# One more step between the up and the down matmuls of an expert tile, TensorE's loop turned each 24 tiles, and the expert output in four PSUM banks

## The reference, cut to what matters

```python
x = x + xattn(layernorm(x), ctx)                # per batch of 128 rows
xt = layernorm(x)                               # 2048 tokens
scores = softmax(xt @ Wg.T)                     # 16 experts; 2 of 4 groups, then the top 4
combine = the scores of the 4 chosen experts
h = silu(xt @ W1[e].T) * (xt @ W3[e].T)         # 176 hidden features
y = sum over e of combine[:, e] * (h @ W2[e].T)
z = silu(xt @ Ws1.T) * (xt @ Ws3.T) @ Ws2.T     # 352 shared hidden features
return x + y + z
```

## Time and profile before

| | us |
|---|---|
| median of 3 executions | 466.83 |
| lowest, highest | 464.65, 470.10 |
| the profiled execution | 459.79 |
| its span, first to last instruction | 457.8 |
| first up matmul of the expert pass | 256.9 |
| start of the last y on ScalarE | 416.4 |

### The profile page before, as it was taken

The page is one execution under the profiler, slowest core; times in us unless marked ns, Lnnn a source line. Parts: engine busy times, 40 slices in busy tenths (PEclk is TensorE's granted clock), DMA queues, the critical chain, the costliest instruction groups (busy, mean ns, idle before and its releaser), DMA issues.

```text
span 457.8 us, 9903 instructions
## 1 busy us (share of the span) xinstructions
PE 332.7 (73%) x2379; PEld 229.9 (50%) x2380; DVE 275.3 (60%) x976; ACT 210.1 (46%) x553; POOL 235.2 (51%) x284
## 2 busy tenths in 40 slices
PE   0788897977888732575099797988988798897830
PEld 0565575655566521243066465665656566574510
DVE  4488879867886883552044454555545455563686
ACT  2466765555454422331145354555555445564510
POOL 2567765588888888717500054554554445453000
PEclk9998766566555555887589999999999989999975
DMA  8713123133333342317340155555555545512994
GB/s 291 246 57 102 64 62 103 56 120 106 119 106 106 115 150 108 116 67 257 124 84 0 32 125 134 126 128 114 125 131 123 118 114 131 129 42 61 348 349 161
DMA packets 82055, 57.79 MB, mean 126 GB/s; under 512 B 58858, under 2 KB 75501, under 8 KB 82032
## 3 DMA queue, kind: packets, MB, share of 16 engines
q1 hardware_dynamic: 63600, 39.60, 30.6%
q0 software_dynamic: 6912, 17.84, 11.0%
q10 hardware_dynamic: 11520, 0.09, 1.5%
HBM read 24.58 MB, written 24.53 MB: 107 GB/s over the span
## 4 chain that ended last, share of the span: by engine, by line
PE 44%; POOL 17%; DVE 12%; issue 12%; another core or an unknown queue 5%; DMA 5%; ACT 2%; SPq 1%; DVEq 0%; POOLq 0%; ACTq 0%
PE bank L715 18%; PE bank L730 12%; POOL slot_rows L1351 6%; DVE x_all L1278 4%; PE bank L723 3%; POOL v L1331 3%; DMA x_all<-x_dram 3%; POOL r L1333 2%; PE bank L721 2%; DMA w<-ranked 2%; PE bank L597 2%; POOL x_all L1313 2%; PE bank L642 1%; PE bank L623 1%
## 5 line engine op out<-in xcount | busy, mean ns | idle before, releaser
L1378 POOL DMA_INDIRECT ranked<-ctx_all x80 | 79.1, 989 | 114.5 <-ACT ctx_all L576 75.4
L730 PE MATMUL bank<-w,hT 128*128 (+3 forms) x560 | 82.3, 280 | 11.2 <-DVE hT L1263 5.8
L715 PE MATMUL bank<-w,ctx_all 128*128 x480 | 85.5, 315 | 1.6 <-issue 1.3
L1351 POOL DMA_INDIRECT slot_rows<-rows_all,slot_k x64 | 65.4, 1021 | 25.6 <-issue 16.7
L1145 DVE SCALAR_TENSOR_TENSOR hid<-bank,silu 128x176 f32<-128x176 f32 x112 | 38.2, 341 | 67.1 <-ACT silu L528 42.9
L528 ACT ACTIVATE silu<-bank 128x176 f32<-128x176 f32 x112 | 35.4, 316 | 75.5 <-PE bank L715 32.2
L730 PEld LDWEIGHTS bank<-w,hT 128*128 128x128 f16 (+1 forms) x560 | 52.5, 100 | 29.9 <-issue 16.5
L533 ACT ACTIVATE hh<-hid 128x176 f16<-128x176 f32 x112 | 39.0, 348 | 39.4 <-DVE hid L1145 31.2
L721 PE MATMUL bank<-hal,hh 128*128 128x128 f16 x112 | 25.2, 225 | 41.5 <-DVE hh L1150 22.5
L715 PEld LDWEIGHTS bank<-w,ctx_all 128*128 128x128 f16 x480 | 43.0, 98 | 20.8 <-issue 3.4
L1263 DVE COPY hT<-bank 128x384 f16<-128x384 f16 x80 | 28.6, 357 | 36.7 <-PE bank L723 22.1
(11 more groups left out here) (139 smaller groups left out, 607.4 us busy)
## 6 DMA issues: line engine op xcount, KB each, us to landing
wst<-w_dram SPq DMA_DIRECT2D x18, 608.0 KB
w<-ranked SPq DMA_DIRECT2D x16, 512.0 KB, 8.8
slot_rows<-pad_rows SPq DMA_DIRECT2D x17, 144.0 KB
x_all<-x_dram SPq DMA_DIRECT2D x4, 512.0 KB, 7.9
out_dram<-x_all SPq DMA_DIRECT2D x4, 512.0 KB, 4.2
ctx_all<-ctx_dram SPq DMA_DIRECT2D x1, 1536.0 KB, 10.7
ctx_all<-slot_rows SPq DMA_TRANSPOSE x80
ctx_all<-slot_rows ACTq DMA_DIRECT2D x80, 1.0 KB
```

The source lines that it names most:

```text
L715: i = mm(U[j][:, 0:UP1], xt(2 * part + k), w[:, span(wcol + wpart * WH + k * UP1, UP1)], start=k == 0 and (wpart, part) == (0, 0), stop=k ...
L730: i = mm(y[:, 0:T], hT[0:rows, j, k * P:(k + 1) * P], w[0:rows, span(col, T)], start=start and n == 0, stop=stop and n == len(parts) - 1)
L1351: G.indirect_dma_start(scatter_rows, bass.IndirectOffsetOnAxis(ap=slot_k[:, b * TOPK + k:b * TOPK + k + 1], axis=0), rows32[:, b * ROW32:( ...
L1378: G.indirect_dma_start(ranked, bass.IndirectOffsetOnAxis(ap=pair(m)[1], axis=0), y_sb[:, m % YR, :], None, bounds_check=(TOPK + 1) * TOKEN ...
```

## The change

Four things change in the expert pass:

- **PE's order**: step s is now D of tile s-4, T of tile s-3, U of tile s. The drain is four steps.
- **PE's loop**: its body is 24 steps (`LONG = 3 * MR`), three passes; the other engines keep bodies of eight steps. The second `weights.load` of a pass (for the tiles four back) is still at the pass's first step alone.
- **Y has four banks**, one for each tile modulo 4, so that the drain's wait of D on y is dropped.
- **ACT** does y of tile s-4 ahead of the address load and of the high half of tile s-1 (it was y of s-3, behind it). **DVE** does the low half of s-2 ahead of the `hT` copy of s-3 (it was behind it).

```diff
-        LAG = {"hlo_ready": 3, "hT_ready": 3}
+        LAG = {"hlo_ready": 3, "hT_ready": 4}
...
-        BODY = MR
-        assert (NT - 2 * RING) % BODY == 0 and BODY % MR == 0 and NT % MR == 0 and 2 * RING == MR
-
-        def expert_pipeline(eng, step, lags=3):
+        LONG = 3 * MR
+        assert (NT - 2 * RING) % LONG == 0 and NT % MR == 0 and 2 * RING == MR
+
+        def expert_pipeline(eng, step, lags=3, body=MR):
             for s in range(2 * RING):
                 step(s, s, None)
-            with eng.Fori(2 * RING, NT - BODY + 1, BODY) as i:
-                for v in range(BODY):
+            with eng.Fori(2 * RING, NT - body + 1, body) as i:
+                for v in range(body):
...
-        U, H, Y = [TP, GP], [SP_, PT], [TS, HO]
+        U, H, Y = [TP, GP], [SP_, PT], [TS, HO, XB, LB]
...
                 if has(s, 1):
                     gate(EX, s - 1, k)
+                if has(s, 4):
+                    t = s - 4
+                    m = (step_v - 4) % YR
+                    wait(act, y_out[m], 4 * (t - m))
+                    act.wait_ge(meta_in[m], 4 * (t - m) + 16)
+                    act.wait_ge(EX["dn_mm"], t + 1)
+                    A(y_sb[:, m, :], Y[m][:, 0:T], ACT.Copy, scale=pair((step_v - 4) % MR)[0]).then_inc(EX["y_ready"], 1)
                 if has(s, 0) and step_v % 4 == 0:
                     pairs.load(s, step_v)
                 if has(s, 1):
                     hidden_high(EX, s - 1, k)
-                if has(s, 3):
-                    t = s - 3
...
-                    A(y_sb[:, m, :], Y[k][:, 0:T], ACT.Copy, scale=pair((step_v - 3) % MR)[0]).then_inc(EX["y_ready"], 1)
...
+                if has(s, 4):
+                    ready("hT_ready", 4)
+                    down(EX["dn_mm"], v % 2, Y[v], weights.of[step_v - 4], start=True, stop=True)
                 if has(s, 3):
                     ready("hlo_ready", 3)
-                    transpose_hidden(EX["ht_mm"], k)
-                if has(s, 1):
-                    m = (step_v - 1) % MR
-                    pe.wait_ge(xt_in[m], 2 * (s - 1 - m) + 16)
-                    wait(pe, EX["h_ready"], s - 2)
-                    up(EX["up_mm"], k, lambda q: xT[:, m, q, :], weights.of[step_v - 1])
-                if has(s, 3):
-                    ready("hT_ready", 3)
-                    if r is None and s >= NT:
-                        pe.wait_ge(EX["y_ready"], s - 4)
-                    down(EX["dn_mm"], k, Y[k], weights.of[step_v - 3], start=True, stop=True)
-
-            expert_pipeline(pe, estep)
+                    transpose_hidden(EX["ht_mm"], 1 - v % 2)
+                if has(s, 0):
+                    m = step_v % MR
+                    pe.wait_ge(xt_in[m], 2 * (s - m) + 16)
+                    wait(pe, EX["h_ready"], s - 1)
+                    up(EX["up_mm"], v % 2, lambda q: xT[:, m, q, :], weights.of[step_v])
+
+            expert_pipeline(pe, estep, 4, LONG)
...
+                if has(s, 2):
+                    hidden_low(EX, s - 2, v % 2, RS["hlo_ready"][(v - 2) % RING], 16)
                 if has(s, 3):
                     dve.wait_ge(EX["ht_mm"], s - 2)
                     wait(dve, EX["dn_mm"], s - 4)
                     V.tensor_copy(hT[:, k, :], H16[k]).then_inc(RS["hT_ready"][(v - 3) % RING], 16)
-                if has(s, 2):
-                    hidden_low(EX, s - 2, v % 2, RS["hlo_ready"][(v - 2) % RING], 16)
```

More of the change, by code:

```diff
@@ L569, in estep @@
                     hidden_high(EX, s - 1, k)
-                if has(s, 3):
-                    t = s - 3
-                    m = (step_v - 3) % YR
-                    wait(act, y_out[m], 4 * (t - m))
-                    act.wait_ge(meta_in[m], 4 * (t - m) + 16)
-                    act.wait_ge(EX["dn_mm"], t + 1)
-                    A(y_sb[:, m, :], Y[k][:, 0:T], ACT.Copy, scale=pair((step_v - 3) % MR)[0]).then_inc(EX["y_ready"], 1)
                 if has(s, 0):
@@ L582, in _ @@
             act.wait_ge(S["table_ready"], 1)
-            expert_pipeline(act, estep)
+            expert_pipeline(act, estep, 4)
             shared_units(act, sstep, B1, B, 1, lambda stage, n: None)
@@ L783, in estep @@
                 v = step_v % RING
-                k = (v + 1) % 2
                 def ready(name, lag):
```

## The result

The changed kernel takes 468.64 us (median of 12 runs) against 466.39 us of the kernel before in the same call: ratio 1.0079, 95% interval 1.0049 to 1.0109. The ratio is of executions outside a slower state that some fall into, so it isn't that of the medians. The kernel is slower by 0.8%, inside the 1% that the prediction called no change, and 20 us above the 449.0 that it forecast. The profiled execution spans 465.9 us, with the same 2379 matmuls.

What follows compares the result with a forecast made beforehand. The expert pass, led by PE's up and down matmuls, was taken to bound the kernel. Hidden loads 3, turns 11 and late signals 4 made 18 us less: 466.8 - 18 = 449 us, range 441 to 459.

Steps and rivals of the forecast that it cites:

- The late signals: PE's transpose signals reaching DVE's `hT` copy late, cause unknown: 8.9 us in the pass, half taken as won, 4 us.
- The pace: PE's up matmuls follow each other in 1.61 us; 80 tiles make 129 us, the pass's other 31 us can be won.
- Single loads hidden: PE's mid-pass address loads hide behind U, 0 to 0.1 us each where they cost 0.35: 3 us less.
- turns: PE's loop entry and two branches back cost 3 us together, where nine times 1.6 us made 14.4: 11 us less.
- Rival A: Low half, `hT`, `hid` and high half on DVE and ACT set the pace, 1.7 us a tile: 456 us, chance 0.15.
- Rival B: PE's single address loads aren't hidden, the sequencer needing 0.3 us more before U: 454 us, chance 0.08.
- Rival C: PE's long loop leaves the instruction buffer; two branches back fetch, 2 us each: 453 us, chance 0.08.
- case C in full: All of PE's long loop fetched late in every pass, twelve fetches in three passes: 461 to 473 us, chance 0.04.
- SP as the next bound: SP's loads need 1.50 us of its own per tile, not much below the new pace of 1.61 to 1.75.

## Why the prediction was wrong

**The step that failed is "The late signals".** It read: "Nothing in the diff names them. Bound from both sides: all stay (0 us won) or all go (8.9 us won) ... I take half, 4 us." A wait with an unknown cause was bounded as if it could only stay or go; that it could grow got 0.05 together with other cases. It grew: from 159.9 - 149.8 = 10.1 us of the pass before (8.9 was the estimate, and its size was about right) to 166.2 - 136.3 = 29.9 us after. That is 19.8 us more where the sum had 4 less, so 24 us of error in the pass; the time was off by 20. By the medians the growth is smaller, from 466.84 - 450.93 = 15.9 us to 468.64 - 438.62 = 30.0 us, as the profiled execution of the kernel before was one of its quicker ones; the sign is the same.

**What the rows could have said.** The prediction used POOL's scatters for their 983 ns and saw that y's wait for them had 6.4 us to spare. The same row gives 263.2 to 417.7 for 80 of them, 1.96 us apart, which is the pass's 159.9 / 80 = 2.0. Whatever happens once a tile has that distance, so the row alone doesn't name the scatters; a run without them does. The pass before was already at the mean distance that the scatters were never seen to go far below, 1.88 to 2.16 us in 14 kernels. The change took some 13 us of turns and loads out of PE's own time, and the scatters did not come more often; the time went into held signals.

**The pace.** 80 x 1.61 = 129 us, and what lies above it can be won: PE does stream at 1.61 us a step in every kernel with whole ups, and without scatters the pass is 136.3. Right about PE, wrong as a bound of the kernel.

**Single loads hidden, 3 us; turns, 11 us.** Right, 14 us together; without scatters the two passes differ by 13.5 us. The parts are right too, from one D to the next against 1.61 us in the runs without scatters. The mid-pass load of the kernel before costs 308.92 - 306.92 - 1.61 = 0.39 us (the prediction had 0.35), and now nothing. A turn there costs 316.72 - 313.76 - 1.61 = 1.35 us (1.6). A turn of the long loop costs 312.76 - 310.47 - 1.61 = 0.68 us and, as the down matmuls behind it take 0.73 instead of 0.55 us, 314.59 - 312.76 - 1.61 = 0.22 us more, together 0.9 (1.2). The turns were taken somewhat too dear on both sides.

**Rival A, the ring on DVE and ACT.** It didn't set the pace: steps of 1.61 us follow each other, and in the kernel without scatters they do for 37 us on end between two turns. Whether it would hold a PE that needs less than 1.61 us, as in the run with short ups, isn't shown.

**Rival B, loads not hidden.** No: the load at 311.2 has no gap beside it.

**Rival C, fetches.** 12 packets instead of 9 in the whole kernel, where case C in full had twelve in the three passes alone. The queues from 320 to 420 us of the changed kernel, all of them:

```profile
q1 hardware_dynamic: 22745, 5.48, 26.3%
q0 software_dynamic: 2400, 5.37, 15.9%
q10 hardware_dynamic: 7200, 0.05, 4.0%
```

PE's second pass ends at 367.5 us and its third at 416.6, and in both there is no fetch. So the loop of some 900 instructions stays inside, and what a turn costs, 0.9 us, is not a fetch. Of the two figures of the Trainium skill that the prediction weighed (Runtime: NRT & Kernel Launch, Instruction fetch mechanics), PE's buffer of 2048 instructions agrees with this trace, and a stall at a branch out of the current two blocks of 256 doesn't.

**SP** as the next bound didn't come into play: in the run without scatters the steps are at 1.61 us with its transposes in place.

**What stays open.** How a scatter holds a signal of another engine isn't shown. That the indirect scatters make PE's signals late is shown by leaving them out, by half their number and by the plain writes. That they do so when one follows within some 1.7 us of another is what the count over the traces says; whether it is their distance as such, or work behind each that isn't done yet, is not shown. Nor do these runs explain why the late signals cost the kernel before, whose PE runs at the same 1.61 us between its turns and loads, only a third as much by the passes and half as much by the medians. The long loop alone, at 1.7% and with its scatters 2.07 us apart, isn't explained either.

## What to carry to other kernels

Ask for each engine and queue what its mean distance is, not only how long one instruction takes. If a thing that happens once a tile comes at about the pass's own pace, cut it out in one run before making another engine faster; here that run said what eight others had only circled. And a wait whose cause isn't known can grow under a change as well as go: its range is open on both sides.

## What the runs showed of the hardware

- Indirect scatters from POOL's queue, 0.98 us each on POOL, make the end signals of PE's matmuls late when one follows closely on another: beside scatters under 1.7 us behind the one before, 273 of 394 `hT` copies came late, beside the others 6 of 403. The latest signals behind a late copy came 2.05 us late in the changed kernel, and 2.77 us with the old orders of ACT and DVE. No lateness of ACT's and DVE's signals shows. Half the rows (0.91 us on POOL) do the same; plain writes of the same bytes (0.54 us) don't, at 1.65 us apart; scatters 2.5 us apart or 3.3 us on average leave next to no gaps (1.8 and 4.1 us, turns among them).
- Beside indirect scatters some semaphore updates of PE, ACT and DVE have no record in the trace (159 of 409 of ACT and DVE between 262 and 400 us of the changed kernel). Without scatters, and with plain writes, none of PE's 240 is missing.
- A matmul's end in the profile and its signal are two things. The Trainium skill (Perfetto Trace Analysis, Tensor Engine Instruction) says that the profiled end is an estimate and that the signal goes out once PSUM has acknowledged the writes. The runs agree that the two differ: by 0.01 us as a rule, and by up to 2.8 us beside scatters. Which of the stages between them takes the time they don't show.
- Held signals show in the profile as "issue" in the chain and as idle time "<-issue" of whoever reads PE's result, or as a long wait for PE's matmul, as the 1.42 us before. An "issue" of over a microsecond ahead of a copy that should be ready was a held signal in this kernel, and not an instruction that was slow to come.
